# The order of the expert loads: gate and up weights ahead of the rows, and an earlier read of row numbers and gates

## The reference, cut to what matters

```python
scores = softmax(x2d @ wg_router.T)                  # 1024 tokens, 32 experts
topk_w, topk_idx = top_k(scores, 6)                  # six experts for each token
C = 2 * (T * 6 // E)                                 # 384 places for each expert
xe = zeros((E, C, 256)).at[flat_idx, safe_pos].add(x_rep)    # tokens sorted by expert
g = einsum('ecd,edf->ecf', xe, w_gate)               # 256 -> 176
u = einsum('ecd,edf->ecf', xe, w_up)                 # 256 -> 176
ye = einsum('ecf,efd->ecd', silu(g) * u, w_down)     # 176 -> 256
y = sum(ye[flat_idx, safe_pos] * topk_w)             # back to the tokens, weighted
return y + sh                                        # sh: a dense expert for all tokens
```

## Time and profile before

| | us |
|---|---|
| median of 3 runs | 940.91 (937.13 to 1130.36) |
| the profiled execution | 940.09 |
| its span, first to last instruction | 938.2 |
| TensorE busy | 782.5 (83% of the span) |
| VectorE busy | 640.7 (68%) |
| ScalarE busy | 507.5 (54%) |
| GpSimd busy | 420.7 (45%) |

### The profile page before, as it was taken

The page is one execution under the profiler, slowest core; times in us unless marked ns, Lnnn a source line. Parts: engine busy times, 40 slices in busy tenths (PEclk is TensorE's granted clock), DMA queues, the critical chain, the costliest instruction groups (busy, mean ns, idle before and its releaser), DMA issues.

```text
span 938.2 us, 17865 instructions
## 1 busy us (share of the span) xinstructions
PE 782.5 (83%) x4618; PEld 665.6 (71%) x4618; DVE 640.7 (68%) x2206; ACT 507.5 (54%) x1283; POOL 420.7 (45%) x319
## 2 busy tenths in 40 slices
PE   6887696889999456798999988999978799998972
PEld 5464576888888344577888867888867688887861
DVE  3563645676776586879768698887855676676753
ACT  2232234777777523565565655555633476777761
POOL 3106574766676513313123131317445076666571
PEclk9997699999999777999999999999989999999995
DMA  9953845887887510000000000002224487888665
GB/s 352 427 213 114 323 145 184 224 215 199 223 215 203 128 61 1 1 2 1 1 1 1 1 1 1 18 1 85 85 78 162 140 220 185 197 221 217 178 146 169
DMA packets 65990, 125.25 MB, mean 133 GB/s; under 512 B 12759, under 2 KB 36951, under 8 KB 64271
## 3 DMA queue, kind: packets, MB, share of 16 engines
q1 hardware_dynamic: 42463, 96.24, 30.8%
q0 software_dynamic: 23472, 28.36, 14.2%
HBM read 75.25 MB, written 53.87 MB: 138 GB/s over the span
## 4 chain that ended last, share of the span: by engine, by line
PE 41%; DVE 28%; issue 12%; DMA 9%; ACT 6%; POOL 2%; DVEq 1%; SPq 1%; ACTq 0%; POOLq 0%
PE bank L329 8%; PE bank L331 7%; PE bank L330 7%; DMA raw<-in_w_gate_up 4%; PE bank L866 3%; DVE over L1765 3%; DVE halves L1588 3%; PE bank L901 3%; DMA over<-token_rows 2%; PE bank L697 2%; DVE over L1727 2%; DVE over L1721 2%; POOL token_rows L1902 2%; PE bank L601 2%; DVE ss L1735 2%
## 5 line engine op out<-in xcount | busy, mean ns | idle before, releaser
L329 PE MATMUL bank<-halves 88*128 88x256 f32 (+2 forms) x548 | 189.3, 345 | 33.8 <-DVE halves L1588 18.3
L331 PE MATMUL bank<-halves 88*128 88x256 f32 (+2 forms) x548 | 169.8, 310 | 0.0
L330 PE MATMUL bank<-halves 88*128 88x256 f32 (+2 forms) x548 | 169.6, 310 | 0.0
L329 PEld LDWEIGHTS bank<-halves 128*128 128x128 f32 (+1 forms) x548 | 105.8, 193 | 53.4 <-issue 39.5
L1902 POOL DMA_INDIRECT token_rows<-xn,slot_ids x96 | 98.5, 1026 | 87.2 <-issue 60.2
L330 PEld LDWEIGHTS bank<-halves 128*128 128x128 f32 (+1 forms) x548 | 106.7, 195 | 1.0
L331 PEld LDWEIGHTS bank<-halves 128*128 128x128 f32 (+1 forms) x548 | 105.4, 192 | 1.1
L1570 DVE TENSOR_TENSOR over<-over,bank 128x176 f32<-128x176 f32 x128 | 42.6, 333 | 66.0 <-ACT over L1093 65.3
L1989 POOL TENSOR_TENSOR over<-over 128x512 f32<-128x512 f32 x16 | 20.6, 1287 | 138.4 <-DVE over L1727 138.4
L1922 POOL DMA_INDIRECT sums_even<-over,row_ids x32 | 56.7, 1773 | 53.4 <-issue 33.7
L1113 ACT ACTIVATE over<-bank,gates 128x256 f32<-128x256 f32 x128 | 60.7, 474 | 33.0 <-PE bank L331 16.3
(11 more groups left out here) (211 smaller groups left out, 2025.4 us busy)
## 6 DMA issues: line engine op xcount, KB each, us to landing
raw<-in_w_gate_up SPq DMA_DIRECT2D x69, 352.0 KB, 3.9
over<-token_rows SPq DMA_DIRECT2D x64, 320.0 KB, 3.2
token_rows<-over SPq DMA_DIRECT2D x10, 1536.0 KB, 21.2
raw<-in_w_down SPq DMA_DIRECT2D x69, 176.0 KB
over<-in_w_qkv_b SPq DMA_DIRECT2D x1, 4096.0 KB, 14.3
raw<-in_w_shared SPq DMA_DIRECT2D x6, 384.0 KB, 9.6
w_out_b_sb<-in_w_out_b SPq DMA_DIRECT2D x1, 2048.0 KB, 39.0
token_rows<-xn,slot_ids POOLq DMA_INDIRECT x96, 2.5
```

What stands on the lines that cost most here:

```text
L329: nc.tensor.matmul(out, hi, rhs_lo, start=start, stop=False)
L330: nc.tensor.matmul(out, lo, rhs_hi, start=False, stop=False)
L331: return nc.tensor.matmul(out, hi, rhs_hi, start=False, stop=stop)
```

## The change

In `expert_traffic` the calls for each expert are put in another order: `gate_up`, `rows`, `down` in place of `rows`, `gate_up`, `down`. In VectorE's `pair` the call of `take` moves from behind the low half of the down weights to just behind the low half of the gate and up weights; in the lines ahead of the first pair it moves ahead of `split_down` too. No instruction is added or removed, and no wait is changed.

```diff
             for e in range(2):
+                gate_up(e + 2, e)
                 rows(e + 2, e)
-                gate_up(e + 2, e)
                 down(e + 2, e)
             with sp.Fori(1, E // 2 - 1) as k:
                 for par in range(2):
                     e = 2 * k + par
+                    gate_up(e + 2, par)
                     rows(e + 2, par)
-                    gate_up(e + 2, par)
                     down(e + 2, par)
@@ pair, VectorE
                     if m == 0 and not (end and par):
                         split_rows(k + par, 1 - par, early and par == 0)
                         split_gate_up(k + par, 1 - par, early and par == 0)
+                        take(k + par, 1 - par)
                     if m == 1 and not (end and par):
                         split_down(k + par, 1 - par, early and par == 0)
-                        take(k + par, 1 - par)
 
             split_gate_up(0, 0, early=True)
             split_rows(0, 0, early=True)
+            take(0, 0)
             split_down(0, 0, early=True)
-            take(0, 0)
```

## The result

The changed kernel takes 952.55 us (median of 4, 947.98 to 953.08); the kernel before took 943.59 on the same chip. The ratio is 1.012, 95% interval 1.008 to 1.016: slower by more than the noise, though by less than the 2% from which the prediction speaks of a change, and 43 us above the 910 us forecast. The profiled execution of the changed kernel spans 951.2 us against 938.2.

The account below looks back on a forecast made before the run. ScalarE's wait for the gate and up weights was taken to set the pace. A 4.61 us step (4.43 TensorE plus 0.18 addition waits) gains 12.5 and 17.7 us in the two layers: 940.1 - 30.2, so 910 us, range 897 to 932.

Parts of the forecast that it names:

- What bounds the kernel, and what `gate_up`'s wait is worth: ScalarE's L1069 waits 39.2 us for the gate and up weights; removing that wait is worth at most 39.2 us.
- The sum: Step forecast for both layers: TensorE's 4.43 us plus 0.18 for remaining addition waits, 4.61 us, giving 910 us.
- the 41.3 us of waiting: Waiting in the 58 steps of both layers, 297.7 us less 58 steps at TensorE's 4.42.
- The `rows` load: SyncE's load issued 0.52 us behind `gate_up`, landing at most 4.5 us later; loop 4.2 us an expert, little room.
- The early `take`: On VectorE, two small instructions moved earlier; 0.14 to 0.3 us hidden by L1598's idle time, counted as nothing.
- What is late next: Loop of the additions to the sums on GpSimd and ScalarE: 4.13, 4.70 or 5.42 us an expert; present waits kept.
- L: Time from the end of the second addition's issue to the waiting L1113: 3.58 us, extremes 2.45 and 5.01; expected to fall.
- its own sign of being wrong: The prediction is wrong if the step stays above 4.75 us though L1069 doesn't wait.
- A: Rival: the additions' loop takes over at 4.93 us a step, gain 12 us, 928 us; chance 0.20.
- C: Rival: fuller DMA engines slow the additions' landing to 5.01 us, loop 5.64 us, time 970 us; chance 0.09.
- B: Rival: rows land late for TensorE; at 6.2 us to landing nothing is gained, 935 to 940 us; chance 0.08.
- Turns between the queues: DMA engines serve queues in turn, so additions' landing would stay at 3.58 us: step 4.70 us, about 915 us.

Follow-up runs that it names:

- e3: Changed kernel with four result buffers, so ScalarE waits for the additions four experts back, not two: 911.84 us, 0.971 of the kernel before.
- e5: Changed kernel with the additions cut to row 0 of the sums: 934.76 us, 0.995 of the kernel before.
- e1: Kernel before with SyncE's order alone changed, `gate_up` ahead of `rows`, `take` left where it was: 941.31 us, ratio 1.000.
- e13: Changed kernel with `gate_up` and `rows` held until ScalarE's high half of the down weights: 944.28 us, 1.003 of the kernel before.
- e12: Kernel before with early `take`, old load order, loads held until ScalarE's high half of the down weights: 936.64 us, ratio 0.991.

## Why the prediction was wrong, point by point

- **What bounds the kernel, and what `gate_up`'s wait is worth: right.** L1069's wait went from 39.2 us to under 1, and once the additions don't hold the step it is 4.61 us (e3). That this is the sum's number is partly luck. The sum took 4.43 us for TensorE (its row has 4.42) and 0.18 for the additions; e3 has no wait for the additions, and TensorE alone is busy for 4.51 us of its step. The 4.42 was one short step standing for all: in the kernel before TensorE was busy for 133.76 / 29 = 4.61 us on average, and the shortest mean step here is e5's 4.53. So the 41.3 us of waiting were put too high.
- **The `rows` load: right in size.** Issued 0.57 us behind `gate_up` (0.52 forecast), median landing 4.2 us ("at most 4.5"), and TensorE doesn't wait for it in the changed kernel. Its slack was rightly called little: e1 and e13 show it gone.
- **The early `take`: right.** L1598 still waits for L1076, 13.3 us in layer 0 (12.4 before), and TensorE waits 5.6 us for L1570 in the two stretches together, 8.5 before.
- **What is late next: wrong, and this is the step that failed.** The prediction said that the loads "leave the second addition's place" and that L would "fall rather than rise", and left the additions' waits at 0.18 us of a step. They measured 99.9 / 58 = 1.72 us. It compared the loads' new time with the additions' old one, in a timeline in which both would move, and it took being issued earlier for being out of the way. ScalarE's wait removed, the loop of the additions has a fixed phase to L1588: the second issue starts inside it and ends 1.42 us behind it, while the loads that wait for `ewlo` are issued 0.2 and 0.7 us behind the very same instruction. Seen from the end of the second issue the loads have moved nearer, from 2.90 and 2.38 us ahead to 1.25 and 0.68. Before, they were almost through when the second addition came; now it has nearly all of their 672 KB ahead of it, and L is 4.30 us in place of 3.56: 0.37 us of a step. What the prediction named as its own sign of being wrong, a step above 4.75 us though L1069 doesn't wait, is what the profile shows.
- **A term that was missing.** The second issue was put at its 1.55 us. It grew to 2.06 (1.63 on average before) for the same reason of phase, 0.2 us of a step. Together 0.59; ScalarE gives back 0.24 by writing the two results in 1.30 us rather than 1.78.
- **The rivals.** A named the loop that took over, with 0.20, but kept L at 3.58 us and so had a gain, 928 us. C named the mechanism and the point from which it decides, L over 4.0 to 4.4 on average, and got 0.09. It took the engines' fullness as the cause; e3, with the fullest engines and a step of 4.61 us, and e12 show that it was the order in time. Its 970 us came from L = 5.01 with 1.75 us for the results. B's late rows didn't come with both edits, only in e1 and e13; its 6.2 us to landing give a step of 5.05 by its own sum, not 5.13.
- **Turns between the queues.** The Trainium skill, "DMA: Bandwidth & Descriptors", section "Queues, rings and completion order", has an engine take turns between its queues, a packet at a time, and the prediction drew from it that L would stay at 3.58 us and the time be 915. L rose, and in 1.8 us none of the addition's packets ran between the 209 of the loads, 13 for each of 16 engines. The section puts some 9 to 17 descriptors into one packet; if what the profile counts as a packet is a descriptor, 13 are about one turn, and there is no conflict. No run here shows which it is. Nor does one show whether the engines could have served the addition earlier. With no loads at all at the end of the kernel before, the additions' queue moves nothing from the end of an issue at 905.05 us to 905.60, and 144 packets from 905.60 to 906.80. So the start alone explains 0.6 us of the 1.9, not the rest, unless the loads slow it down too. (The 2.45 us of the earlier trace rows were not wholly free of loads: 0.06 MB of them still moved from 900.12 to 902.57 us.)

## What to carry to other kernels

When an edit removes the wait that sets the pace, the loop behind it takes over with a phase of its own: work out where its pieces fall relative to the signal that now releases the loads, and don't read their place off the old timeline. Two loops of nearly the same length hide each other, so an edit to one is worth nothing, or less, until the other has a buffer more; here the early `take` and two more result buffers give 0.970, and neither alone gives anything. Loads that are issued as early as possible can be too early, if a shorter transfer on the critical loop has to queue behind them.

## What was not expected of the hardware

- While the loads' queue was busy (88% of the 16 engines) the additions' queue moved nothing for 1.8 us, and L followed the bytes ahead of it: 0.6 us for 176 KB. With no loads it was silent for 0.6 us behind the end of an issue.
- An indirect DMA's issue on GpSimd that starts inside a VectorE instruction with two SBUF inputs lasts until 1.42 us behind that instruction's end: 1.55 us when free, 2.13 when it starts 0.17 us into L1588, 1.77 or 2.13 with that in two halves.
